# A selective scan on one core: du times B for two blocks in one GpSimd instruction, six buffers for it, and a carry copied one beat later

## The reference, cut to what matters

```
x_in, res = split(x @ W_in);  u = silu(causal_conv4(x_in) + b)
dt, B, C  = split(u @ W_x);   delta = softplus(dt @ W_dt + b_dt)
for every token:  h[d, n] = exp(delta[d] * A[d, n]) * h[d, n] + delta[d] * B[n] * u[d]
                  y[d]    = sum over n of h[d, n] * C[n]  + D[d] * u[d]
x  = layernorm(x + (y * silu(res)) @ W_out)
x  = layernorm(x + (silu(x @ Wg) * (x @ Wu)) @ Wd)
```

## Time and profile before

| | |
|---|---|
| median of 3 runs | 1873.07 us (1872.35 to 1873.95) |
| span of the profiled execution | 1865.8 us, 32487 instructions |
| median less span | 7.3 us |
| TensorE | 1715.3 us (92%) |
| VectorE | 1705.4 us (91%) |
| GpSimd | 1651.8 us (89%), of which 1310.6 us in 1024 products dbu |
| ScalarE | 1636.9 us (88%) |
| mean granted TensorE clock | 0.979 |

### The profile page before, as it was taken

One profiled execution on the slowest core, in us unless ns is written; L12 is line 12 of the kernel. 1 busy time (PEld: TensorE's weight loads), 2 busy tenths in 40 slices (PEclk: granted clock), 3 DMA queues, 4 the chain that ended last, 5 costly groups with the idle time before them and its releaser, 6 DMA issues.

```text
span 1865.8 us, 32487 instructions
## 1 busy us (share of the span) xinstructions
PE 1715.3 (92%) x10128; PEld 1287.3 (69%) x10128; DVE 1705.4 (91%) x1958; ACT 1636.9 (88%) x2769; POOL 1651.8 (89%) x1629
## 2 busy tenths in 40 slices
PE   8879898998989999898998989999898998988788
PEld 3546676776767677676776767677676776767667
DVE  5989999999999999999999999999999999999994
ACT  5798988989899898998989899898998989898774
POOL 3989899998989989899898999989899898989970
PEclk9999999999999999999999999999999999999999
DMA  7213123141231314214141231313214041221100
GB/s 240 109 46 136 47 71 134 35 159 47 103 102 58 125 47 142 63 60 145 35 151 55 99 106 58 125 47 135 70 58 147 36 147 57 87 96 41 62 23 24
DMA packets 82107, 164.56 MB, mean 88 GB/s; under 512 B 10369, under 2 KB 28033, under 8 KB 81938
## 3 DMA queue, kind: packets, MB, share of 16 engines
q1 hardware_dynamic: 80498, 160.90, 25.1%
q10 hardware_dynamic: 1440, 1.58, 0.3%
HBM read 87.47 MB, written 8.91 MB: 52 GB/s over the span
## 4 chain that ended last, share of the span: by engine, by line
PE 65%; ACT 22%; POOL 7%; issue 4%; DVE 2%; DMA 0%; DVEq 0%; SPq 0%; ACTq 0%; POOLq 0%
PE fill L524 10%; PE ht_upper L699 9%; PE ht_lower L699 9%; PE y_upper L724 8%; PE fill L639 8%; POOL dbu L1185 6%; PE fill L608 5%; PE fill L629 5%; ACT da L1052 4%; ACT gt L1061 3%; PE fill L539 3%; ACT L1140 2%; ACT L1129 2%; PE fill L578 2%; ACT kb L948 2%
## 5 line engine op out<-in xcount | busy, mean ns | idle before, releaser
L1185 POOL TENSOR_TENSOR dbu<-du,brep 128x512 f32<-128x512 f32 x1024 | 1310.6, 1306 | 152.3 <-DVE h L1360 128.7
L1360 DVE TENSOR_TENSOR_SCAN h<-da,carry,dbu 128x512 f32<-128x512 f32 x960 | 1186.9, 1269 | 92.5 <-ACT da L1052 90.7
L1052 ACT ACTIVATE da<-delta,a_s 128x512 f32<-128x512 f32 x960 | 655.7, 689 | 97.2 <-DVE h L1360 89.8
L1061 ACT ACTIVATE gt<-ht_upper,ct 128x512 f32<-128x512 f32 x512 | 348.5, 681 | 62.7 <-PE ht_upper L699 55.7
L699 PE MATMUL ht_upper<-ident,h 128*128 128x128 f32 x2048 | 317.7, 278 | 67.7 <-DVE h L1360 57.3
L699 PEld LDWEIGHTS ht_upper<-ident,h 128*128 128x128 f32 x2048 | 245.9, 143 | 185.9 <-DVE h L1360 102.8
L1372 DVE SCALAR_TENSOR_TENSOR acc<-ht_lower,ct,acc 128x512 f32<-128x512 f32 x480 | 348.6, 726 | 22.4 <-PE ht_lower L699 22.4
L699 PE MATMUL ht_lower<-ident,h 128*128 128x128 f32 x2048 | 317.0, 278 | 39.4 <-DVE acc L1372 34.9
L724 PE MATMUL y_upper<-ident,gt 128*128 128x128 f32 x2048 | 316.6, 278 | 0.0
L699 PEld LDWEIGHTS ht_lower<-ident,h 128*128 128x128 f32 x2048 | 243.8, 143 | 103.0 <-issue 50.4
L724 PEld LDWEIGHTS y_upper<-ident,gt 128*128 128x128 f32 x2048 | 245.8, 143 | 72.1 <-ACT gt L1061 39.6
(11 more groups left out here) (189 smaller groups left out, 1871.9 us busy)
## 6 DMA issues: line engine op xcount, KB each, us to landing
brep<-b_rows SPq DMA_DIRECT2D x127, 512.0 KB, 3.8
xs<-xin SPq DMA_DIRECT2D x242, 256.0 KB, 2.5
xr<-x SPq DMA_DIRECT2D x16, 512.0 KB, 4.2
xt_s<-x_t SPq DMA_DIRECT2D x15, 512.0 KB, 5.1
out<-xr SPq DMA_DIRECT2D x15, 512.0 KB, 3.9
win_s<-w_in SPq DMA_DIRECT2D x2, 512.0 KB, 5.0
h<-xin SPq DMA_DIRECT2D x4, 256.0 KB, 4.0
h<-xin ACTq DMA_DIRECT2D x4, 256.0 KB, 4.5
```

The source lines that it names most:

```text
L1052: nc.scalar.activation(dst[:, :], delta[:, par, m, :], ACT.Exp, scale=a_s[:, m, n:n + 1])\
L1061: nc.scalar.activation(gt[:, (n * UPPER + k) % GT, :], ht_upper[:, :], ACT.Copy, scale=ct[:, par, k, n:n + 1])\
L1185: nc.gpsimd.tensor_tensor(dbu[:, beat % DBU, :], du[:, par, m, :], brep[:, n // PIECE % 2, n % PIECE, :], ALU.mult).then_inc(dbu_ready, 1)
L1360: nc.vector.tensor_tensor_scan(h[:, n % 2, m, 0:T], da[beat % 2][:, :] if slot is None else da_ahead[:, slot, :], dbu[:, beat % DBU, :], c ...
```

## The change

GpSimd is given one instruction at every even beat, which makes the products of blocks m and m+1 into two neighbouring buffers (the row of B is read for both by a step of 0). It waits for two blocks of du at n = 0, and for scan `beat-5` (h_ready of beat+2-6). `dbu` has six buffers, and as 64 is no multiple of six, the buffer goes by the count over all chunks. The copy of state n's carry now stands ahead of the pair of beats 4n+8 and 4n+9 and has a wait of its own, for scan 4n+3. `gt` has three buffers; the four columns of `direct_w`, used only at the start, move to the end of another one.

```diff
--- before.py
+++ after.py
@@ -45,7 +45,7 @@
 
 UPPER = LOWER = 2
 TURN_AT, WEIGH_AT, ADD_AT, BACK_AT = (4, 4, 6, 7), (5, 7), (5, 7), (7, 9)
-GT = 4
+GT = 3
 
 
 READ_AT = {"conv0": 14, "conv1": 20, "conv2": 22, "conv3": 26, "ct": 48, "down0": 55, "down1": 57, "down2": 63,
@@ -74,7 +74,7 @@
 STORE_AT = max(BEAT["norm"][1] + 1 - 64, 0)
 AHEAD = 2
 SILUS = sorted(BEAT[name] for name in ("silu uz", "silu gate"))
-SAVE_AT = 3
+SAVE_AT = 0
 assert all(b - a > AHEAD + 1 for a, b in zip(SILUS, SILUS[1:]))
 
 assert not [n for n, at in READ_AT.items() if n[:2] == "dt" and n != "dtb" and at - 1 in SILUS]
@@ -129,7 +129,7 @@
     XD = P
     GROUP = P // KCONV
     GROUPS = P // GROUP
-    DBU = 4
+    DBU = 6
 
     x_flat = x.rearrange("r d -> (r d)")
     out_flat = out.rearrange("r d -> (r d)")
@@ -187,7 +187,7 @@
         eye = gt[:, 0, 0:GROUP]
         convw_s = gt[:, 1, 0:DB * GROUPS].rearrange("p (m g) -> p m g", m=DB)
 
-        direct_w = gt[:, 3, 0:KCONV]
+        direct_w = gt[:, 1, DI - KCONV:DI]
         direct_d = gt[:, 2, :].rearrange("p (k d) -> p k d", k=KCONV)
         kb = sb("kb", [P, HB, T])
         xr = sb("xr", [P, 2, TT, DM])
@@ -1177,13 +1177,15 @@
             def times_b(i, par, beat):
                 n, m = beat // DB, beat % DB
                 if n == 0:
-                    pool.wait_ge(du_ready, i * DB + m + 1)
+                    pool.wait_ge(du_ready, i * DB + m + 2)
                 if n % PIECE == 0 and m == 0:
                     piece = n // PIECE
                     pool.wait_ge(b_loaded[piece % 2], 8 * NB * i + 16 * (piece // 2 + 1))
-                after(pool, h_ready, i * NH + beat + 1 - DBU)
-                nc.gpsimd.tensor_tensor(dbu[:, beat % DBU, :], du[:, par, m, :],
-                                        brep[:, n // PIECE % 2, n % PIECE, :], ALU.mult).then_inc(dbu_ready, 1)
+                after(pool, h_ready, i * NH + beat + 2 - DBU)
+                slot = (i * NH + beat) % DBU
+                row = brep[:, n // PIECE % 2, n % PIECE:n % PIECE + 1, :]
+                nc.gpsimd.tensor_tensor(dbu[:, slot:slot + 2, :], du[:, par, m:m + 2, :], row.broadcast_to([P, 2, T]),
+                                        ALU.mult).then_inc(dbu_ready, 2)
 
             def cast(n, k):
 
@@ -1224,7 +1226,7 @@
             def save_carry(i, n, ends):
 
                 start = T - 1 + ends
-
+                pool.wait_ge(h_ready, i * NH + (n + 1) * DB)
                 nc.gpsimd.tensor_copy(carry[:, n, :], h[:, n % 2, :, start])\
                     .then_inc(carry_saved, 1)
 
@@ -1232,14 +1234,15 @@
                 first, last = [isinstance(i, int) and i == c for c in (0, NCH - 1)]
                 ends, ended = [int(c % PER_SEQ == PER_SEQ - 1) for c in (i, i - 1)]
                 for beat in range(NH):
-                    times_b(i, par, beat)
+                    n = beat // DB - 2
+                    if beat % DB == SAVE_AT and n >= 0:
+                        save_carry(i, n, ends)
+                    elif beat % DB == SAVE_AT and not first:
+                        save_carry(i - 1, NS + n, ended)
+                    if beat % 2 == 0:
+                        times_b(i, par, beat)
                     if first and CAST_AT <= beat < CAST_AT + 2 * WEIGHT_PARTS and (beat - CAST_AT) % 2 == 0:
                         cast(*divmod((beat - CAST_AT) // 2, 3))
-                    n = beat // DB - 1
-                    if beat % DB == SAVE_AT and n >= 0:
-                        save_carry(i, n, ends)
-                    elif beat == SAVE_AT and not first:
-                        save_carry(i - 1, NS - 1, ended)
                     for which in [] if first else tiles_due("shift", beat):
                         shift(i - 1, which)
                     for which in [] if isinstance(i, int) and i < 2 else tiles_due("shift", NH + beat):
@@ -1358,7 +1361,7 @@
 
                 after(dve, carry_saved, i * NS + n - 1)
                 nc.vector.tensor_tensor_scan(h[:, n % 2, m, 0:T], da[beat % 2][:, :] if slot is None
-                                             else da_ahead[:, slot, :], dbu[:, beat % DBU, :],
+                                             else da_ahead[:, slot, :], dbu[:, (i * NH + beat) % DBU, :],
                                              carry[:, n, m:m + 1], ALU.mult, ALU.add).then_inc(h_ready, 1)
 
             def sum_states(i, par, n, k):
```

## The result

In four runs of each, one after the other on one chip, the changed kernel took 1893.01 us (1890.28 to 1895.97) and the kernel before 1873.51 us (1872.35 to 1874.54): a ratio of 1.0106, with a 95% interval of 1.0091 to 1.0121. It is slower by about 19.5 us, where +13 was forecast.

A forecast was written before the change was run, and what follows sets the result against it. No engine alone was taken to bound the kernel; products were early nearly everywhere. 4.1 - 0.5 + 8.4 + 1.0 = +13.0 on span 1865.8 gives 1878.8, with 7.3 around it 1886.1; range 1866 to 1897.

The forecast's parts named there:

- Cost of a pair: GpSimd's product of 1024 columns takes 2.36 us against 2 x 1.28; some 100 us saved, hidden behind scans, worth 0.
- Rival 3: A pair saves nothing (2.56 us), blocks grow and the chunk boundary comes late: 1896, chance 0.14.
- Start: Chunk 0: the pairs wait for two du blocks, so scan 6 comes at 48.7 instead of 44.54: +4.1 us.
- Rest of chunk 0: After the start, cheaper products and six buffers give back a third of VectorE's 1.4 us idle time: -0.5 us.
- The scans that read SBUF: Behind a SiLU, scans 46 and 47 wait for the running GpSimd pair and end 1.0 us later.
- 14 x 0.6 = 8.4: In 14 chunks the late scans 46 and 47 delay ScalarE's weighing by 0.6 us each: +8.4, between 0 and 14.
- Rival 1: The blocks at the scans are absorbed and only the start is paid: +3.6, 1876.7, chance 0.15.
- rival 2: GpSimd was the bound where it has hardly a gap; its lead gives back VectorE idle time: 1867.9, chance 0.21.
- TensorE is full afterwards: Behind scans 46 and 47 TensorE has no room to recover the delay; part of the +8.4 argument.
- Last chunk: Beats 36 and 37, where scan 38 follows at once, so the hold-up of the scans shows: +1.0 us.
- Boundary, gt, copy: Pair (0, 1) at each chunk boundary, three gt buffers and the carry's later copy each cost 0.
- 7.3 us around the span: Difference between the profiled span, 1865.8, and the runs' median, 1873.1, taken to lie around the span and added.

The follow-up runs named there:

- start_hold_again: Changed kernel, first four products single, pairs of beats 40 and 50 held until scans 37 and 47 end; third chip: 1869.97 us, 0.9995 of the kernel before.
- start4: Changed kernel with the first four products of chunk 0 made one by one: 1885.66 us, 1.0071 of the kernel before.
- start_hold: Changed kernel, first four products single, copy and pair of beat 40 held until scan 37 ends, pair of beat 50 until scan 47: 1869.38 us, 0.9985.
- single6: Changed kernel with all products single; six buffers, three gt and the later copy kept: 1876.03 us, 1.0016 of the kernel before.
- series of doses: Kernels compared at one place of a middle chunk, the same hold-up in five sizes: TensorE's wait of 0.99 gives +0.11 us, 1.57 gives +0.70.
- hold50: Changed kernel with the pair of beats 50 and 51 held until scan 47 has ended: 1876.87 us, 1.0025 of the kernel before.
- up1_twice: Changed kernel with tile up1 computed twice, 1.2 us more TensorE work a chunk just ahead of L569: 1886.81 us, 1.0077 of the kernel before.
- gt_save: Kernel before with only three gt buffers and the carry's copy moved ahead of product 4n+8 with its own wait: 1870.68 us, 0.9996.
- before_hold: Kernel before with product 39 held until scan 37 has ended and product 49 until scan 47 has ended: 1870.60 us, 1.0000.
- after: The changed kernel itself, in its first measurement against the kernel before: 1893.01 us, 1.0106.
- after_again: Changed kernel unchanged, measured again on the second chip: 1891.56 us, 1.0096 of the kernel before.
- hold40: Changed kernel with the carry copy and the pair of beats 40 and 41 held until scan 37 has ended: 1887.02 us, 1.0080 of the kernel before.
- pairs4: Changed kernel with four dbu buffers instead of six: 1932.07 us, 1.0327 of the kernel before.

## Why the prediction held, step by step

Slower was forecast, 1886 in a range of 1866 to 1897, and 1893.0 came; the mechanism is shown, the size 6.5 us short.

- *Cost of a pair*, 2.36: 2.375, and its saving hidden behind the scans: held, by start_hold_again. The repeated row of B costs nothing. Rival 3 falls.
- *Start*, scan 6 at 48.7: 49.49. The order of steps was the one forecast, each a little later (du 3 done at 41.0, not 40.7; scan 3 at 46.06, not 45.5), and scan 6 came 3.4 us behind scan 3 in place of the 3.2 taken over from before (44.54 less 41.40 are 3.14), with TensorE's clock at half from 39.8 to 50.1. *Rest of chunk 0*, -0.5: of +4.95 there was +4.20 left at scan 36. 3.6 forecast, 4.2 measured; start4 bears it out within a wide interval, start_hold by its scan 36 (91.11).
- *The scans that read SBUF*, +1.0 for two scans: 3.17 to 4.21. The release by scan 45 and the 0.4 us of lead are in the rows. The Trainium skill ("SBUF — State Buffer", "Who interferes with whom") says that the holder keeps the shared pair for its whole instruction: agreed, scan 46 was held up for 1.76 us of the 1.95 that the pair still ran, and the series of doses grows with the instruction. It also says that issue order decides who blocks; scan 36 of single6 does not bear this out beyond the running instruction, since three products that began behind it (91.81, 93.18 and 94.42) passed it over.
- *14 x 0.6 = 8.4*: the period rose by 0.66, 9.2 in all. Rival 1 (absorbed) and rival 2 (GpSimd was the bound) fall by hold50 and start_hold_again. The 0.6 was argued from ScalarE being busy until 227.81; the doses show the same slack more plainly.
- **The term that was mis-sized**: these 14 chunks cost 13 to 15 us, not 8.4. "TensorE is full afterwards" took its speed as given. The idle time ahead of L569 tripled, and in 3 to 5 of 14 chunks the clock fell behind it, 1.4 us each, 4 to 7. up1_twice takes away just that and leaves the block; hold50 takes away both. Most of the 6.5 us by which the forecast was short is this.
- *Last chunk*, +1.0: 1.1 or nothing, by the clock; the rest of its 2.7 in this profile was the clock too: +0.7 ahead of scan 36 and +0.8 behind scan 46, both where it fell.
- *Boundary, gt, copy*, 0: held. POOL waits 63.1 us for the softplus (0.2 in the kernel before), as the step said it must.
- *7.3 us around the span*: wrong as a name, right as a sum. 1.8 lie around; the rest was that profile's luck. Kernels as fast as before have profiles of 1873.5 (gt_save) and 1871.1 (before_hold): in both some 3 us more are idle time ahead of L539 (six and five times, not once) and 1.6 a fall of the clock at the start of chunk 1, in gt_save 2.4 more a longer fall in the last chunk.

Open: what decides in which chunks the clock falls, and what TensorE waits for ahead of L539.

## What to carry to other kernels

Where two engines hold each other up at SBUF, as GpSimd's products and the scans with both inputs there do, what counts is the length of one instruction and not the load: before making an instruction of the idler engine longer, look which instructions of the other start while it runs, and either hold it back to their end (hold50, one line, at no cost) or leave it short there. The stall on TensorE had a free part here (0.9 us), then a part that counted one for one, and at 1.57 us half the clock behind it in some chunks, so a wait of 0.5 us that "costs nothing" is not a measure of what 1.6 will cost. And compare one profile's span with the runs before taking it for typical.

## What was not expected of the hardware

- With 0.63 us of idle time at the same place the clock kept its level in 14 of 14 chunks, with 1.57 it fell to 1.2 GHz in 3 to 5 of 14 in four executions (after, after_again, hold40, start4); for TensorE's products at L578 that is 2.05 against 1.10 us.
- A scan with two SBUF inputs can be held up across several GpSimd instructions that follow each other without a gap: 5.84 us in place of 1.27, once per span, in single6. In the kernel before the same place in chunk 0 shows 3.23 us: there one product passed it over, then it got in, and the copy that stood next took 1.12 us in place of 0.23. What decides between the two is open.
- It works both ways: a copy of four columns on GpSimd takes 0.19 us, and 1.11 beside a scan with both inputs in SBUF (pairs4).
- A product with a repeated row, 1024 columns, takes 2.373 us, 2.1 ns a column beyond the 0.2 us of a small one: the fixed part is what a pair saves, 0.18 us of 2.56.
